# First stage of an attention and binary-FFN layer: rotated projections in a two-part split

## The reference

```python
xn = _layernorm(x, axis=-1)
split = lambda t: t.reshape(b, n, H, Dh).transpose(0, 2, 1, 3)   # H = 16, Dh = 16
q, k, v = (split(xn @ W + bias) for W, bias in ((Wq, bq), (Wk, bk), (Wv, bv)))
q, k = _rope(q), _rope(k)          # x * cos + rot * sin, rot = pairs (x1, x2) -> (-x2, x1)
weights = softmax(q k^T / sqrt(256))
attn = (weights @ v) merged over heads, @ Wo + bo
h = relu(s0 * [xn, -xn] @ sign(k0)) * 2
h = relu(s1 * h @ sign(k1)) * 2
out = x + attn + s2 * h @ sign(k2)
```

## Time and profile before

| | |
|---|---|
| median of three runs | 2800.49 us |
| profiled execution, its own time | 2802.49 us |
| its span in the trace | 2800.7 us |
| `prepare`: first projection to the end of `fill` | 20.07 to 325.86 us |
| `attend`: first score multiply to the end | 357.24 to 2800.7 us |
| period of a chunk in `prepare` | 18.7 us |
| mean granted clock of TensorE | 0.977 |

### The profile page before, as it was taken

How to read it: one execution, slowest core, us unless ns; L and a number is a source line. 1 busy time by engine, 2 the same in 40 slices (tenths; PEclk the granted TensorE clock), 3 DMA queues, 4 the chain that set the end, 5 groups by cost and what they waited for, 6 DMA issues and landing times.

```text
span 2800.7 us, 49497 instructions
## 1 busy us (share of the span) xinstructions
PE 2638.2 (94%) x20423; PEld 1330.8 (48%) x20423; DVE 1087.2 (39%) x1689; ACT 2105.5 (75%) x2301; POOL 378.1 (14%) x309
## 2 busy tenths in 40 slices
PE   6777289999999999999999999999999999999997
PEld 3334144444444545454545455454545454545444
DVE  7999632323242423323332323242323323332323
ACT  4445268888888887878787878888787878787883
POOL 4888500000000000000000000000000000000000
PEclk9988689999999999999999999999999999999998
DMA  6666521212121222212222212131222212221313
GB/s 197 194 195 203 153 61 40 65 39 61 35 65 41 67 56 56 71 50 68 54 73 58 73 39 83 35 85 41 65 65 53 70 46 73 58 73 43 84 27 109
DMA packets 279701, 211.74 MB, mean 76 GB/s; under 512 B 183616, under 2 KB 227392, under 8 KB 272960
## 3 DMA queue, kind: packets, MB, share of 16 engines
q1 hardware_dynamic: 271040, 200.30, 26.3%
q10 hardware_dynamic: 8448, 8.39, 0.9%
...
## 4 chain that ended last, share of the span: by engine, by line
PE 79%; ACT 5%; issue 2%; DMA 1%; SPq 0%; DVE 0%; POOLq 0%; POOL 0%; DVEq 0%
PE ps_o L909 33%; PE ps_f L944 23%; PE ps_s L894 21%; ACT probs L874 5%; PE ps_f L957 2%; DMA xT<-xn_t 0%; PE ps_f L999 0%; DMA probs<-rest_sum_d 0%; DVE k_rows L1113 0%; PE ps_o L999 0%; SPq L789 0%; DMA heads_t<-heads 0%; SPq L691 0%; POOLq L703 0%; POOL heads L1018 0%
## 5 line engine op out<-in xcount | busy, mean ns | idle before, releaser
L874 ACT ACTIVATE probs<-ps_s 128x1024 f32<-128x1024 f32 x2048 | 1945.3, 1032 | 482.0 <-PE ps_s L894 471.3
L909 PE MATMUL ps_o<-probs,v_ones 128*32 128x512 f32 x8192 | 1011.8, 600 | 0.0
L894 PE MATMUL ps_s<-q_rows,k_rows 50*128 50x512 f32 x4096 | 859.4, 440 | 38.0 <-DMA q_rows<-row_shift 33.4
L894 PEld LDWEIGHTS ps_s<-q_rows,k_rows 50*128 50x128 f32 x4096 | 367.7, 184 | 687.6 <-ACT probs L874 599.3
L1073 DVE TENSOR_SCALAR h_hi<-ps_f 128x512 fp32r<-128x512 f32 x224 | 154.4, 689 | 921.8 <-PE ps_f L944 921.8
L944 PE MATMUL ps_f<-h_hi,ffn_w 64*128 64x512 f32 x2048 | 409.0, 394 | 0.0
L944 PE MATMUL ps_f<-h_lo,ffn_w 64*128 64x512 f32 x2048 | 406.6, 391 | 0.0
L909 PEld LDWEIGHTS ps_o<-probs,v_ones 128*32 128x32 f32 x8192 | 200.7, 109 | 427.0 <-issue 330.8
L1018 POOL TENSOR_TENSOR heads<-heads,sums 128x512 f32<-128x512 f32 x64 | 82.6, 1291 | 2169.5 <-DVE sums L1039 2169.5
L1039 DVE RECIPROCAL sums<-sums 128x128 f32<-128x128 f32 x256 | 228.4, 925 | 1.1
L944 PEld LDWEIGHTS ps_f<-h_lo,ffn_w 64*128 64x128 f32 x2048 | 196.3, 186 | 36.8
...
## 6 DMA issues: line engine op xcount, KB each, us to landing
k_rows<-k_parts SPq DMA_DIRECT2D x128, 256.0 KB
...
k_rows<-k_parts SPq DMA_DIRECT2D x128, 128.0 KB
...
```

The costliest lines, as they stand in the source:

```text
L874: nc.scalar.activation(probs[:, s % PBUF, half * 2 * C:(half + 1) * 2 * C], ps_s[:, half].rearrange("p c n -> p (c n)"), ACT.Exp, scale=SC ...
L894: last = nc.tensor.matmul(ps_s[:, half, w], k_rows[rows, u, t * P:(t + 1) * P], q_rows[rows, u, half], start=True, stop=True)
L909: last = nc.tensor.matmul(ps_o[32 * c:32 * c + 2 * DH], v_ones[:, u, t], probs[:, s % PBUF, c * C:(c + 1) * C], start=(t == 0), stop=(t == ...
```

## The change: what it does

- The normalised chunk is split while it is in `ps_t`: ACT writes the high part `x_hi` (L351 of the changed kernel), DVE the low part `x_lo` (L560). Both go to DRAM, where one float32 array went before.
- The weights are split once, at the start, into high and low parts, and a second copy of Wq and Wk has neighbouring columns exchanged. DVE makes the high parts, POOL the low ones; PE's first projection waits for them (`w_split`).
- `project` multiplies each block by the plain and by the exchanged weights, each as three float32r products (high x high, high x low, low x high) for each half of the contraction: 12 multiplies a block, where there were 2 in float32. `values` makes v the same way, 24 multiplies of 256 columns a chunk, where there were 8 in float32. v is summed in `ps_t`.
- DVE's `products` (L552, L554) add the bias and multiply by cos and sin straight out of `ps_p`; the swap and `qk` are gone. POOL adds the two products (L503). ACT squares the rotated block (L359) and copies its high part (L362), POOL subtracts for the low part (L496). `parts` has four buffers, `turned` three.
- The order of the work is written anew on all engines, without `Fori`. The FFN's sign work on DVE is at the end of chunk 1. The memory of `fill` serves as the zeros too.
- `attend` loads `xT_hi` and `xT_lo` from DRAM, at head j = 1 of a pass (before: `xT` at j = 2), and DVE's `split` is gone; `carry` has memory of its own.

```diff
--- before.py
+++ after.py
-ADDED = 2
+PART_BUFS = 4
...
-        xnT = sb("xnT", [P, 2, DT, C], F32)
+        x_hi = sb("xn_hi", [P, 2, DT, C], F32R)
+        x_lo = sb("xn_lo", [P, 2, DT, C], F32R)
...
+        wqk_hi = sb("wqk_hi", [P, 2, 2, DT, D], F32R)
+        wqk_lo = sb("wqk_lo", [P, 2, 2, DT, D], F32R)
...
+        by_sin = sb("by_sin", [P, 2, C], F32)
+        turned = sb("turned", [P, 3, C], F32)
+        parts = sb("parts", [P, PART_BUFS, PARTS, C], F32R)
+        square = sb("square", [P, 2, 4, C], BF16)
...
+        ps_p = ctx.enter_context(nc.psum_tensor("ps_p", [P, 2, 2, C], F32))
+        ps_n = ctx.enter_context(nc.psum_tensor("ps_n", [P, C], F32))
+        ps_v = ps_t[:].rearrange("p k n -> p (k n)").rearrange("p (t d) -> p t d", d=D)
...
+            def store_x(c):
+                u = c % 2
+                sp.wait_ge(x_split, c + 1)
+                sp.dma_start(hi_out[c], x_hi[:, u].bitcast(F32)).then_inc(x_stored[u], 16)
+                sp.dma_start(lo_out[c], x_lo[:, u].bitcast(F32)).then_inc(x_stored[u], 16)
+            def store_parts(n):
+                b, r, j = n // (4 * CB), n // 4 % CB, n % 4
+                u = n % PART_BUFS
+                sp.wait_ge(parts_ready, n + 1)
+                sp.dma_start((q_out if j < DT else k_out)[b, j % DT, r], parts[:, u].bitcast(F32)).then_inc(parts_stored[u], 16)
+            store_x(0)
+            for c in range(NC):
+                if c > 0:
+                    store_parts(4 * c - 1)
+                sp.wait_ge(v_ready, c + 1)
+                sp.dma_start(v_out[c // CB, c % CB], v_sb[:, c % 2].rearrange("p h t d -> p h (t d)")).then_inc(v_stored[c % 2], 16)
+                store_parts(4 * c)
+                store_parts(4 * c + 1)
+                if c + 1 < NC:
+                    store_x(c + 1)
+                store_parts(4 * c + 2)
+            store_parts(4 * NC - 1)
...
+            def high(c):
+                u = c % 2
+                act.wait_ge(xn_turned, c + 1)
+                if c >= 2:
+                    act.wait_ge(x_stored[u], 32 * (c // 2))
+                nc.scalar.activation(x_hi[:, u].rearrange("p k n -> p (k n)"), ps_t[:].rearrange("p k n -> p (k n)"),
+                                     ACT.Copy).then_inc(x_high, 1)
+            def part(n):
+                c, j, u = n // 4, n % 4, n % PART_BUFS
+                act.wait_ge(turn_done, n + 1)
+                if j == 0 and c >= 2:
+                    act.wait_ge(norm_done, c - 1)
+                nc.scalar.activation(square[:, c % 2, j], turned[:, n % 3], ACT.Square).then_inc(square_ready, 1)
+                if n >= PART_BUFS:
+                    act.wait_ge(parts_stored[u], 16 * (n // PART_BUFS))
+                nc.scalar.activation(parts[:, u, 0], turned[:, n % 3], ACT.Copy).then_inc(part_high, 1)
...
+            load_x(0)
+            load_x(1)
+            deviation(0)
+            normalise(0)
+            high(0)
+            deviation(1)
+            act.wait_ge(weights_loaded, 16 * 6)
+            for c in range(NC):
+                if c > 0:
+                    part(4 * c - 1)
+                values(c)
+                if c + 1 < NC:
+                    normalise(c + 1)
+                part(4 * c)
+                part(4 * c + 1)
+                if c + 1 < NC:
+                    high(c + 1)
+                if c + 2 < NC:
+                    deviation(c + 2)
+                part(4 * c + 2)
+                if c == NC - CB:
+                    act.wait_ge(d0_ready, 1)
+                    act.wait_ge(signs_ready, 1)
+                    act.wait_ge(ffn_loaded, 16 * 6)
+                if c >= NC - CB:
+                    ffn_weights(c % CB)
+            part(4 * NC - 1)
...
+            def project(n):
+                c, j = n // 4, n % 4
+                u = c % 2
+                if n == 0:
+                    pe.wait_ge(w_split, 1)
+                if j == 0:
+                    pe.wait_ge(x_split, c + 1)
+                if n >= 2:
+                    pe.wait_ge(products_ready, n - 1)
+                for swapped in range(2):
+                    for k in range(DT):
+                        at = slice((j % DT) * P, (j % DT + 1) * P)
+                        w_hi, w_lo = wqk_hi[:, swapped, j // DT, k, at], wqk_lo[:, swapped, j // DT, k, at]
+                        to = ps_p[:, n % 2, swapped]
+                        nc.tensor.matmul(to, w_hi, x_hi[:, u, k], start=(k == 0), stop=False)
+                        nc.tensor.matmul(to, w_hi, x_lo[:, u, k], start=False, stop=False)
+                        last = nc.tensor.matmul(to, w_lo, x_hi[:, u, k], start=False, stop=(k == DT - 1))
+                last.then_inc(proj_ready, 1)
+            def values(c):
+                u = c % 2
...
+            turn(0)
+            for c in range(NC):
+                project(4 * c)
+                values(c)
+                if c > 0:
+                    lengths(c - 1)
+                project(4 * c + 1)
+                project(4 * c + 2)
+                if c + 1 < NC:
+                    turn(c + 1)
+                project(4 * c + 3)
+            lengths(NC - 1)
...
+            pool.wait_ge(weights_loaded, 16 * 6)
+            pool.wait_ge(w_high, 1)
+            nc.gpsimd.tensor_tensor(wqk_lo[:, 0], wqk[:], wqk_hi[:, 0].bitcast(F32), ALU.subtract)
+            plain, crossed = (x.rearrange("p n k (m two) -> p n k m two", two=2) for x in (wqk[:], wqk_hi[:, 1]))
+            crossed_lo = wqk_lo[:, 1].rearrange("p n k (m two) -> p n k m two", two=2)
+            for side in range(2):
+                nc.gpsimd.tensor_tensor(crossed_lo[..., side], plain[..., 1 - side], crossed[..., side].bitcast(F32), ALU.subtract)
+            nc.gpsimd.tensor_tensor(wv_lo[:], wv[:], wv_hi[:].bitcast(F32), ALU.subtract).then_inc(w_split, 1)
+            def low(n):
+                pool.wait_ge(part_high, n + 1)
+                p = parts[:, n % PART_BUFS]
+                nc.gpsimd.tensor_tensor(p[:, 1], turned[:, n % 3], p[:, 0].bitcast(F32), ALU.subtract).then_inc(parts_ready, 1)
+            for n in range(4 * NC):
+                u = n % 2
+                pool.wait_ge(products_ready, n + 1)
+                if n >= 3:
+                    pool.wait_ge(parts_ready, n - 2)
+                nc.gpsimd.tensor_tensor(turned[:, n % 3], by_cos[:, u], by_sin[:, u], ALU.add).then_inc(turn_done, 1)
+                if n > 0:
+                    low(n - 1)
+            low(4 * NC - 1)
...
+            def products(n):
+                c, j, u = n // 4, n % 4, n % 2
+                dve.wait_ge(proj_ready, n + 1)
+                if n >= 2:
+                    dve.wait_ge(turn_done, n - 1)
+                nc.vector.scalar_tensor_tensor(out=by_cos[:, u], in0=ps_p[:, u, 0], scalar=bqk[:, 0, j:j + 1], in1=cos[:, here(c)],
+                                               op0=ALU.add, op1=ALU.mult)
+                nc.vector.scalar_tensor_tensor(out=by_sin[:, u], in0=ps_p[:, u, 1], scalar=bqk[:, 1, j:j + 1], in1=sin[:, here(c)],
+                                               op0=ALU.add, op1=ALU.mult).then_inc(products_ready, 1)
+            def low(c):
+                u = c % 2
+                dve.wait_ge(x_high, c + 1)
+                nc.vector.tensor_tensor(x_lo[:, u].rearrange("p k n -> p (k n)"), ps_t[:].rearrange("p k n -> p (k n)"),
+                                        x_hi[:, u].rearrange("p k n -> p (k n)").bitcast(F32), ALU.subtract).then_inc(x_split, 1)
...
+            dve.wait_ge(weights_loaded, 16 * 6)
+            nc.vector.tensor_copy(wqk_hi[:, 0], wqk[:])
+            plain = wqk[:].rearrange("p n k (m two) -> p n k m two", two=2)
+            crossed = wqk_hi[:, 1].rearrange("p n k (m two) -> p n k m two", two=2)
+            for side in range(2):
+                nc.vector.tensor_copy(crossed[..., side], plain[..., 1 - side])
+            nc.vector.tensor_copy(wv_hi[:], wv[:]).then_inc(w_high, 1)
+            nc.vector.stream_shuffle(bqk[:, 1], bqk[:, 0], [i ^ 1 for i in range(32)]).then_inc(bias_swapped, 1)
+            low(0)
+            sums(1)
+            factors(1)
+            nc.vector.tensor_copy(per_head[:], per_head_f[:]).then_inc(consts_ready, 1)
+            nc.vector.memset(fill[:].bitcast(F32), 0.0).then_inc(zero_ready, 1)
+            nc.vector.memset(ones[:], 1.0)
+            dve.wait_ge(tables_loaded, 32)
+            dve.wait_ge(bias_swapped, 1)
+            for c in range(NC):
+                products(4 * c)
+                if c > 0:
+                    keep_norms(c - 1)
+                products(4 * c + 1)
+                if c + 2 < NC:
+                    sums(c + 2)
+                products(4 * c + 2)
+                if c + 1 < NC:
+                    low(c + 1)
+                products(4 * c + 3)
+                if c + 2 < NC:
+                    factors(c + 2)
+                if c == 1:
+                    dve.wait_ge(ffn_loaded, 16 * 6)
...
+            def load_x(i):
```

(11 more changed lines are left out.)

391 lines of the change are left out of this document (122 added, 269 removed).

## The result

| | before | changed |
|---|---|---|
| median | 2800.52 us (2798.3 to 2802.43, 4 runs) | 2763.6 us (2763.0 to 2764.13, 4 runs) |
| ratio, 95% interval | | 0.9868 (0.9851 to 0.9885) |
| profiled execution, its own time | 2802.49 us | 2764.13 us |
| its span | 2800.7 us | 2762.3 us |
| first projection to the end of `fill` | 20.07 to 325.86 us | 18.55 to 289.70 us |

The kernel is faster by 1.3%, 36.9 us by the medians and 38.4 us by the profiled executions. The forecast was 2762 us as a median, 38.4 us less than before, within 2750 to 2786. The total is right; its terms are not all, and the experiments show that some of the reasons were not either.

A forecast was written before the change was run, and what follows sets the result against it. DVE bounds `prepare` before, PE after: 14.8 us of work plus 1.1 of wait make 15.9 us a chunk for 18.7. With start and end, `fill` ends 38.4 us earlier: 2764.1 profiled, 2762 us as median, range 2750 to 2786.

The forecast's parts named there:

- What bounds: In `prepare`, DVE sets the pace before at 18.3 of 18.7 us a chunk; PE becomes the bound after.
- PE's multiplies: In `prepare`, 48 of 512 columns at 0.22 us and 24 of 256 at 0.115; PE's sum 14.8 us a chunk.
- The wait of the turn: After transposing the next chunk and finishing the fourth block, PE waits for DVE's `xn_lo`: about 1.1 us with handoffs.
- Start: Start of `prepare`: first projection at 19.6 us for 20.07; half clock makes the first block cost 2.6 us more.
- The sign work: On DVE at the end of chunk 1: takes 5 to 8.5 us, of which 1.9 us on the path.
- End: End of `prepare`: last projection at 277.4 us, then 6.5 and 3.5 us; `fill` ends at 287.4 for 325.86.
- Behind `prepare`: After `fill`, its store, the barrier and the loads are as before; `attend` gains 0 to 1.7 us, taken as 0.
- The 2.0 us taken off for the median: Whole kernel: median of the runs 2.0 us below the profiled execution, so 2764.1 becomes 2762 us.
- The lock chain: Before `xn_lo`, small DVE operations and POOL's subtractions lock each other: 17.1 us a chunk, 19 us more, 2781; chance 0.14.
- the 1.85 of the rival: PE loses its clock at each turn between chunks: 1.85 us each, 28 us more, 2790; chance 0.08.
- whole-array float32r multiplies: In PE's projections, no faster than a float32 record, 0.43 us: 184 us more, 2946, slower; chance 0.04.
- The case of cheap multiplies: In `prepare`, DVE's 11.9 us and the turn's chain bound: some 13.5 us a chunk, 38 us less, 2724; chance 0.03.

The follow-up runs named there:

- the kernel in which PE never waits for `xn_lo`: Changed kernel with DVE's statistics behind `xn_lo`, PE's first block waiting only for weight parts it reads, and ACT making `xn_hi` before block 4c + 1: 2746.8 us.
- The first experiment: Changed kernel with the statistics of chunk c + 2 moved on DVE behind `xn_lo` of chunk c + 1, and ACT's square root one place back: 2753.93 us.
- the kernel with two products: Changed kernel without the product low part of the weights x high part of x in the blocks of q and k: 2745.77 us.
- two edits of order: Changed kernel without weights' low part x high part of x for q and k, statistics behind `xn_lo` on DVE, and `xn_hi` before block 4c + 1 on ACT: 2717.28 us.

## Why the prediction was right, and where it wasn't

- **What bounds.** Right: DVE before, PE after. In the middle chunk PE is busy 15.52 of 16.33 us (forecast: over nine tenths of 15.9), DVE 11.74 (11.9), GpSimd 10.10 (10.2 to 11.5), DMA share 0.88 (0.89).
- **PE's multiplies.** The mis-sized term. I took 0.22 us and 0.115 us; they are 0.229 and 0.12. With 48, 24 and the rest PE issues for 15.36 us a chunk, not 14.8; the kernel in which PE never waits for `xn_lo` has a chunk of 15.25. The Trainium skill (TensorE: Matmul & The Clock Gate, Back-to-back issue gap) gives 131 ns for a multiply of 512 columns in a sustained stream. No float32r multiply of `project` comes near it: 227 ns is the least from start to start.
- **The wait of the turn.** Right in place, cause and size: 1.1 us forecast, 0.97 measured (15.36 to 16.33). The first experiment shows that it was DVE's order. For the end I took off one wait, 1.1 us; but the statistics of the last two chunks are missing, and so is a second wait, and the last chunk has no transposes: 1.7 us less than forecast together.
- **Start.** First multiply at 18.55 for 19.6. Chunk 0 has 18.11 us from its first multiply to the next chunk's, 1.8 more than the others, where I added 2.6. The first block alone lost 2.4 us at half clock (18.55 to 23.74, for 2.75 us); chunk 0 has no lengths to sum. The sign work cost 0.4 us (a chunk of 16.76), not 1.9.
- **End.** These terms together, and 0.4 for the one chunk of 16.70 us: + 0.43 x 16 = 6.9, - 1.05, - 0.8, - 1.5, - 1.7, + 0.4 is + 2.2; the last projection ended 2.2 us later than forecast, at 279.6. From there to the end of `fill` 10.1 us for 10.0. `fill` ended at 289.7 for 287.4.
- **Behind `prepare`.** "As before" was wrong by 1.9 us to the good. The store of `fill` is issued at 289.73, 0.03 us behind `fill`, where it was 0.84; the rest lies in the barrier and the loads. At the start of `attend` PE waits 1.10 us for the second loaded array instead of 1.75 for DVE's queue, and `attend` is 0.3 us shorter: 0, as taken. So 2.3 us too few in `prepare` and 1.9 too many behind it nearly cancel. That the profiled execution has the forecast 38.4 us to the tenth is luck, inside `prepare` too, where 7.3 us too few meet 5.1 too many. The 2.0 us taken off for the median were 0.5, so the median is 1.6 us above the forecast.
- **Rivals.** The lock chain at 17.1 us a chunk didn't come; one small operation a chunk is held up in the chain (L528, 1.29 us), as forecast. The clock didn't fall at the turns (granted 1.00 in the middle chunks, with 0.8 to 1.2 us of idle); it is the kernel with two products that shows it falling, behind waits of 2.6 us, and there it cost 1.5 us a time, near the 1.85 of the rival. Nor are whole-array float32r multiplies dear. The case of cheap multiplies put the next bound at 13.5 us a chunk; with PE cut to 11.7 us the changed order gave 15.25, and 12.98 was reached only after two edits of order.
- **GpSimd and the casts.** The rival weighs GpSimd's hold on DVE by L534, which has two operands in SBUF, and L520, which has one there. The cast L532 has one as well and is held up all the same: 0.40 us free, 0.92 us in the mean and 1.51 behind GpSimd's addition. The Trainium skill (SBUF — State Buffer, Who interferes with whom) says that an instruction with at most one SBUF input doesn't contend with GpSimd, but only outside the modes that use two ports, and it counts casts among the operations that can enter these. I didn't weigh the cast. It changed no term of the sum, since the forecast's products read PSUM and took 0.74 us throughout.
- **What the change is credited with.** The forecast counted from the new kernel's chunk and never asked what part of the old 18.7 us was DVE's work. 1.2 us of it was one cast behind GpSimd, and went with the loops. In the kernel before, writing the loops out alone brings 14.9 us, and one cast on ACT with four buffers, an earlier root and DVE's changed order 20.5 more. That is the whole 36.9 us: 2764.27 and 2763.6 us are the same time, without float32r, exchanged weights or products out of PSUM. Counted the other way, the rebuilding with the parts left on DVE is only 4.3 us below the kernel before with its loops written out (2780.47 for 2784.74), and taking the parts off DVE brings the other 16.9. The rebuilding does have more room: DVE's and ACT's order and the earlier start give it 16.8 us more. What the same care would give the kernel with the cast moved wasn't tried.
